# A spectral layer in 32 units: the inverse transform's last two chunks are moved behind the next unit's first transform

## The reference, cut to what matters

```python
xf = jnp.fft.rfft2(x, axes=(1, 2), norm='ortho')              # x: (4, 128, 128, 768)
xr, xi = xf.real, xf.imag                                     # split in 8 blocks of 96 channels
o1r = relu(xr @ w1[0] - xi @ w1[1] + b1[0])                   # per block, 96x96
o1i = relu(xi @ w1[0] + xr @ w1[1] + b1[1])
o2r = o1r @ w2[0] - o1i @ w2[1] + b2[0]
o2i = o1i @ w2[0] + o1r @ w2[1] + b2[1]
o = softshrink(stack(o2r, o2i), 0.01)
out = jnp.fft.irfft2(o, s=(128, 128), norm='ortho') + x
```

## Time and profile before

| | |
|---|---|
| time, median of 3 runs | 5289.3 us (5289.18 to 5289.44) |
| the profiled execution | 5295.64 us, its span 5293.8 us |
| TensorE matmuls busy | 5047.7 us, 95% of the span |
| VectorE, ScalarE, GpSimd busy | 73%, 56%, 27% |
| mean granted TensorE clock | 0.984 of full |
| the 16 DMA engines | 36% of the span on data |

### The profile page before, as it was taken

How to read it: one execution, slowest core, us unless ns; L and a number is a source line. 1 busy time by engine, 2 the same in 40 slices (tenths; PEclk the granted TensorE clock), 3 DMA queues, 4 the chain that set the end, 5 groups by cost and what they waited for, 6 DMA issues and landing times.

```text
span 5293.8 us, 113159 instructions
## 1 busy us (share of the span) xinstructions
PE 5047.7 (95%) x40128; PEld 4731.8 (89%) x40128; DVE 3859.0 (73%) x6195; ACT 2978.4 (56%) x5384; POOL 1434.6 (27%) x905
## 2 busy tenths in 40 slices
PE   6999999999999999999999999999999999999997
PEld 5999889998899988999989998999998999988996
DVE  4777777777777777777767777777777777777775
ACT  4555655556555556555565555655556655556553
POOL 3033312333123332233331233312333223332120
PEclk8999999999999999999999999999999999999998
DMA  4034432344323444223443234432334422344322
GB/s 109 16 87 101 101 71 53 80 101 101 82 55 79 89 101 100 54 64 86 101 102 68 57 82 98 101 79 61 76 89 101 95 58 65 86 101 101 71 67 61
DMA packets 1699963, 430.22 MB, mean 81 GB/s; under 512 B 1699104, under 2 KB 1699232, under 8 KB 1699360
## 3 DMA queue, kind: packets, MB, share of 16 engines
q1 hardware_dynamic: 1699360, 422.47, 36.1%
HBM read 220.89 MB, written 201.33 MB: 80 GB/s over the span
## 4 chain that ended last, share of the span: by engine, by line
PE 90%; DVE 6%; issue 2%; ACT 1%; SPq 1%; DMA 0%; DVEq 0%; ACTq 0%
PE psum L768 15%; PE psum L742 14%; PE psum L818 13%; PE psum L791 13%; PE psum L724 10%; PE psum L801 9%; PE psum L754 7%; PE psum L830 3%; PE psum L831 3%; PE psum L832 3%; DVE spectrum L633 1%; DVE spectrum L632 1%; DVE mixed L654 1%; DVE x L691 1%; SPq L361 1%
## 5 line engine op out<-in xcount | busy, mean ns | idle before, releaser
L654 DVE COPY mixed<-psum 128x768 f32<-128x768 f32 (+1 forms) x544 | 508.1, 934 | 838.5 <-PE psum L754 838.5
L742 PE MATMUL psum<-w_whole,whole 128*128 128x192 f32 x4160 | 796.6, 334 | 110.1 <-ACT whole L480 101.5
L544 ACT ACTIVATE sums_high<-psum 128x512 fp32r<-128x512 f32 x768 | 458.9, 597 | 727.2 <-PE psum L818 727.2
L768 PEld LDWEIGHTS psum<-mats,mixed 128*128 128x128 f32 x6272 | 744.0, 191 | 121.2 <-issue 112.0
L768 PE MATMUL psum<-mats,mixed 128*128 128x128 f32 x6272 | 841.8, 283 | 0.0
L742 PEld LDWEIGHTS psum<-w_whole,whole 128*128 128x128 f32 x4160 | 684.2, 200 | 130.9 <-ACT whole L480 107.6
L724 PE MATMUL psum<-mats,x 128*128 128x128 f32 x6144 | 725.3, 280 | 65.3 <-DVE spectrum L633 28.7
L724 PEld LDWEIGHTS psum<-mats,x 128*128 128x128 f32 x6144 | 713.0, 196 | 75.7 <-DVE spectrum L633 28.9
L791 PE MATMUL psum<-w2t,hidden 128*128 128x192 f32 x4160 | 768.2, 327 | 0.0
L818 PE MATMUL psum<-mats,spectrum 128*128 128x128 f32 x6144 | 743.4, 275 | 13.2 <-DVE spectrum L661 13.2
L818 PEld LDWEIGHTS psum<-mats,spectrum 128*128 128x128 f32 x6144 | 714.2, 192 | 15.6 <-DVE spectrum L661 15.6
(11 more groups left out here) (83 smaller groups left out, 7491.9 us busy)
## 6 DMA issues: line engine op xcount, KB each, us to landing
x<-x SPq DMA_DIRECT2D x736, 192.0 KB, 2.8
out<-x SPq DMA_DIRECT2D x736, 192.0 KB, 2.4
x<-x SPq DMA_DIRECT2D x736, 64.0 KB, 2.6
out<-x SPq DMA_DIRECT2D x736, 64.0 KB, 2.2
x<-x SPq DMA_DIRECT2D x32, 144.0 KB, 2.7
w2t<-L_conv_w SPq DMA_DIRECT2D x128, 36.0 KB
out<-x SPq DMA_DIRECT2D x32, 144.0 KB, 2.3
x<-x SPq DMA_DIRECT2D x64, 48.0 KB, 2.2
```

The source lines that it names most:

```text
L654: dve.tensor_copy(mixed[s % 2][:, 0:k], both_b(s)[:, 0:k]).then_inc(b_copied, 1)
L742: pe.matmul(bank_b(s, k), whole[s % 2][:, k // 2, :, k % 2], w1_whole[par][:, :, :].rearrange("p r o -> p (r o)"), start=k % 2 == 0, stop= ...
L768: last = pe.matmul(out[tile], flat[:, tile * SIZE:(tile + 1) * SIZE], mat(FH), start=True, stop=True)
```

## The change

Chunks 22 and 23 of stage F are issued after the next unit's stage A and not before it. They go into banks 2 and 3, and VectorE adds them after it has emptied stage A's last group and made its share of the gather. Stage A's group 2 therefore no longer comes after F's chunk 23; it waits for the add of chunk 20, whose bank (7) it now takes, since the banks of stage A are turned by one. Groups 4 and 5 wait for `sums_low` of chunks 22 and 23.

Group 21 of stage A is copied out by ScalarE (13 groups, 26 copies) and no longer by VectorE (11 groups). Of the four last gather copies, the one that ScalarE did second is done by VectorE, at the same time as ScalarE does the first.

The loops turn at other places. TensorE does stage A of unit 0 ahead of its loop; its body begins with the layers, so it turns between F's chunk 23 and stage B. ScalarE and VectorE do stage A and the layers of unit 0 ahead of theirs; their body begins with the inverse, so they turn between the layers and the inverse. All three bodies hold four units and turn seven times, and the last units stand behind. All units but the last now have two groups of the next stage A ahead of their stage E.

```diff
+LATE = 2
+NF = NQ - LATE
+A_ACT = [at for at in range(NA) if at % 2 == 0 or at == NA - 3]
+A_DVE = [at for at in range(NA) if at not in A_ACT]
         def bank_a(at):
-            return bank(2 + at if at < AHEAD else 4 + at % 4)
+            return bank(2 + at if at < AHEAD else 4 + (at + 1) % 4)
         def bank_f(q):
-            return bank(F_BANKS[q % len(F_BANKS)] if q < NQ - 1 else 0)...
+            return bank(F_BANKS[q % len(F_BANKS)] if q < NF else 2 + q - NF)...
# ScalarE, gather(0)
-                    act.activation(w[0:BLOCK, :, slice(*INNER)], parts[0:BLOCK, 0], ACT.Copy)
-                    act.activation(w[BLOCK:SIZE, :, slice(*INNER)], parts[HALF:BLOCK, 1], ACT.Copy).then_inc(whole_gathered, 1)
+                    act.activation(w[0:BLOCK, :, slice(*INNER)], first_parts(*INNER)[0:BLOCK, 0], ACT.Copy).then_inc(whole_gathered, 1)
# VectorE, end of stage A
+                dve.tensor_copy(whole[0][BLOCK:SIZE, :, slice(*INNER)], parts[HALF:BLOCK, 1]).then_inc(early_gathered, 1)
                 dve.tensor_copy(halved[0][0:HALF, slice(*INNER)], parts[0:HALF, 1, 0])
                 dve.tensor_copy(halved[0][HALF:SIZE, slice(*INNER)], parts[0:HALF, 1, 1]).then_inc(first_halved, 1)
# VectorE (ScalarE has the same order, without the adds)
+            def forward_next(n, m, par):
+                forward(n)
+                for q in range(NF, NQ):
+                    add(1 - par, n - 1, q)
+            def body(loop, unit, last=False):
...
+                inverse(1 - par, n - 1)
+                forward_next(n, m, par)
+                layers(m, par, n, False, last)
# TensorE, stage_a
-                    if at == 3:
-                        pe.wait_ge(f_added, n * NQ)
+                    elif end_of is not None and at == AHEAD:
+                        pe.wait_ge(f_added, end_of * NF + (NF - 1))
+                    elif end_of is not None and at > AHEAD + 1:
+                        pe.wait_ge(low_copied, end_of * NQ + (NQ + at - AHEAD - 3))
# TensorE, stage_c
+                if s == 0:
+                    pe.wait_ge(f_late_added, n * LATE)
# TensorE, stage_f
-                if q == NQ - 1:
-                    pe.wait_ge(f_added, n * NQ + (NQ - 2))
-                elif q >= len(F_BANKS):
-                    pe.wait_ge(f_added, n * NQ + (q - len(F_BANKS) + 1))
+                if len(F_BANKS) <= q < NF:
+                    pe.wait_ge(f_added, n * NF + (q - len(F_BANKS) + 1))
+            def late(n):
+                for q in range(NF, NQ):
+                    stage_f(n, q)
+            def body(loop, unit):
...
+                layers(par, n)
+                stage_a(m + par, 1 - par, n + 1, 0, AHEAD)
+                inverse(n)
+                stage_a(m + par, 1 - par, n + 1, AHEAD, NA, end_of=n)
+                late(n)
+            stage_a(0, 0, 0, 0, NA)
+            with pe.Fori(0, PAIRS // UNROLL - 1) as loop:
                 for unit in range(2 * UNROLL):
...
+                    body(loop, unit)
+            for unit in range(2 * UNROLL - 1):
+                body(PAIRS // UNROLL - 1, unit)
+            layers(1, UNITS - 1)
+            inverse(UNITS - 1)
+            late(UNITS - 1)
```

More of the change, by code:

```diff
@@ L494, in gather @@
                 act.activation(h[HALF:SIZE], parts[0:HALF, 1, 1], ACT.Copy).then_inc(halved_gathered, 1)
-            with act.Fori(0, PAIRS // UNROLL) as loop:
-                for unit in range(2 * UNROLL):
[L498 to L544, removed]
@@ new lines, in inverse @@
+            def inverse(n):
+                for q in range(NQ):
+                    act.wait_ge(e_done, n * NQ + (q + 1))
+                    act.activation(sums_high[:, q % RING], bank_e(q), ACT.Copy).then_inc(high_copied, 1)
+            def body(loop, unit, last=False):
+                m, par = loop * UNROLL + (unit + 1) // 2, (unit + 1) % 2
+                n = m * 2 + par
+                inverse(n - 1)
+                forward(n)
+                layers(m, par, n)
+            forward(0)
@@ L546, in _ @@
+            layers(0, 0, 0)
+            with act.Fori(0, PAIRS // UNROLL - 1) as loop:
+                for unit in range(2 * UNROLL):
+                    body(loop, unit)
+            for unit in range(2 * UNROLL - 1):
+                body(PAIRS // UNROLL - 1, unit, last=unit == 2 * UNROLL - 2)
+            inverse(UNITS - 1)
         @block.vector
@@ new lines, in layers @@
+            def layers(m, par, n, first, last):
+                for s in range(NS + 2):
+                    if s < NS:
+                        k = pairs(s)
+                        dve.wait_ge(b_done, n * NS + (s + 1))
+                        dve.tensor_copy(mixed[s % 2][:, 0:k], both_b(s)[:, 0:k]).then_inc(b_copied, 1)
+                    for stage in ("sums", "tiles") if s < NS else ("tiles", "sums"):
+                        if stage == "sums" and s >= 2:
+                            t, rows = s - 2, rows_d(s - 2)
+                            j = 2 + 2 * GROUPS[t][0]
+                            dst = real_kw[:, :, :] if t == REAL else U[:, 0:BLOCK, j:j + rows]
+                            dve.wait_ge(excess_done, n * NS + (t + 1))
+                            dve.scalar_tensor_tensor(dst, parts_d(t), LAMBDA, excess[:, :, 0:rows], op0=ALU.add,
+                                                     op1=ALU.min).then_inc(shrunk, 1)
+                        if stage == "tiles" and 1 <= s <= NS:
+                            t = s - 1
+                            dve.wait_ge(c_done, n * NS + (t + 1))
+                            dve.tensor_scalar(middle[t % 2][:, 0:pairs(t)], middle_c[:, 0:pairs(t)], b1t[par][:, 1:2], 0.0,
+                                              ALU.add, ALU.max).then_inc(middle_done, 1)
+                    if 2 <= s < NS:
+                        k = rows_d(s) // 2
+                        dve.wait_ge(shrunk, n * NS + (s - 1))
+                        dve.tensor_copy(bank_d(s).rearrange("p (k r) c -> p k r c", r=2)[:, 0:k],
+                                        b2_rows[par][:, :, :].unsqueeze(1).broadcast_to([SIZE, k, 2, BLOCK])).then_inc(seeded, 1)
+                    if s < 2 * NP and not first:
+                        unfold_step(n - 1, 1 - par, s)
+                    if 2 * NP <= s < 2 * NP + PREPARE and not last:
+                        prepare_step(m + par, 1 - par, s - 2 * NP)
@@ new lines, in inverse @@
+            def inverse(par, n):
+                for batch in range(0, NQ, BATCH):
+                    for q in range(batch, batch + BATCH):
+                        dve.wait_ge(high_copied, n * NQ + (q + 1))
+                        dve.tensor_tensor(sums_low[:, q % RING], bank_e(q), sums_high[:, q % RING],
+                                          ALU.subtract).then_inc(low_copied, 1)
+                    for q in range(batch - BATCH, batch):
+                        if q >= 0:
+                            add(par, n, q)
@@ L698, in _, with body @@
+            def forward_next(n, m, par):
+                forward(n)
+                for q in range(NF, NQ):
+                    add(1 - par, n - 1, q)
+            def body(loop, unit, last=False):
+                m, par = loop * UNROLL + (unit + 1) // 2, (unit + 1) % 2
+                n = m * 2 + par
+                inverse(1 - par, n - 1)
+                forward_next(n, m, par)
+                layers(m, par, n, False, last)
             for k in range(PREPARE):
                 prepare_step(0, 0, k)
-            turn(0, first=True)
@@ L701, in _ @@
-            with dve.Fori(1, PAIRS // UNROLL - 1) as loop:
-                turn(loop)
-            turn(PAIRS // UNROLL - 1, last=True)
+            forward(0)
+            layers(0, 0, 0, True, False)
+            with dve.Fori(0, PAIRS // UNROLL - 1) as loop:
+                for unit in range(2 * UNROLL):
+                    body(loop, unit)
+            for unit in range(2 * UNROLL - 1):
+                body(PAIRS // UNROLL - 1, unit, last=unit == 2 * UNROLL - 2)
+            inverse(1, UNITS - 1)
@@ L704, in _ @@
+            for q in range(NF, NQ):
+                add(1, UNITS - 1, q)
             for k in range(2 * NP):
@@ L710, in mat, with stage_a @@
                 return mats[:, columns]
-            def stage_a(m, par, n, first, end):
+            def stage_a(m, par, n, first, end, end_of=None):
                 for at, g in list(enumerate(A_ORDER))[first:end]:
@@ L833, in stage_f, with layers, inverse @@
                 last.then_inc(f_done, 1)
+            def layers(par, n):
+                for s in range(NS + 2):
+                    if s < NS:
+                        stage_b_whole(par, n, s)
+                    if s == NS:
+                        flip(n)
+                        stage_c(n, NS - 1)
+                    if s >= 2:
+                        stage_d_outer(par, n, s - 2)
+                        stage_d_middle(par, n, s - 2)
+                    if s < NS:
+                        stage_b_halved(par, n, s)
+                    if 1 <= s < NS:
```

(16 more changed lines are left out.)

193 lines of the change are left out of this document (87 added, 106 removed).

## The result

The changed kernel takes 5331.0 us (median of 4 runs, 5328.8 to 5332.0) against 5289.2 us: the ratio is 1.0079, with an interval of [1.0062, 1.0097], so it is slower by 0.8%. The forecast was 5158 us, and the range went to 5200. So 173 us are to be found.

The account below looks back on a forecast made before the run. TensorE was taken as the bound, so only its waits and lower clock could be won: 83.7 (turns) + 23.5 (clock) + 49 - 27 (loops) + 1.2 + 0.5 (ends) = 131 us off 5289.3, giving 5158; range 5135 to 5200.

Parts of the forecast that it names:

- a turn within the body: From F's chunk 22 to the next stage B: 22.85 us in place of 25.55, 2.70 saved 31 times, 83.7 us.
- The clock: After the gaps before stage B: no more falls to 1.2 GHz, 16 x 1.47 = 23.5 us saved.
- Rival 3: VectorE's late adds, beside GpSimd's halving, delay the layers' first `mixed` copy: slower, 5298 us if 5 us late; chance 0.03.
- the late adds: VectorE's adds of F's late chunks, behind the gather: done about 3.8 us after stage A, 0.5 us of cover left.
- Rival 2: The gap before stage B stays 3.17 us, late F fills 1.4, the clock holds: 5197 us, chance 0.13.
- The late chunks: F's last two chunks, 1.40 us, hide fully in the 1.91 before stage B; group 2 starts after 0.91.
- Group 21 on ScalarE: At stage A's end VectorE is free for group 23, which is out 1.44 us after stage A.
- The loops' turns: Seven old turns at 7.0 us saved, 49 us; six new ones at 2.5 + 1.3 + 0.7 paid, 27 us.
- The 0.7 for the clock: At each of six new loop turns, a 3.03 us gap lets the clock fall half the time: half of 1.47.
- The sum: Whole kernel: 83.7 + 23.5 + 49 - 27 + 1.2 + 0.5 = 131 us saved, giving 5158 us.

Follow-up runs that it names:

- e1: Changed kernel with the second of the last gather copies back on ScalarE; all else of the change stays: 5151.3 us, ratio 0.9735 to the kernel before.
- e2: Changed kernel with GpSimd's halving made to wait until VectorE's gather copy is done: 5140.0 us, ratio 0.9714 to the kernel before.
- e4: Changed kernel with GpSimd's halving cut into two instructions of half the rows: 5169.5 us, ratio 0.9770 to the kernel before.
- e6: Changed kernel with VectorE's 32x132 gather copy made as two copies of 32x66 beside the halving: 5142.4 us, ratio 0.9716 to the kernel before.
- e5: Kernel before with one thing changed, the second of ScalarE's last two gather copies moved to VectorE: 5409.2 us, ratio 1.0223.
- e9: Changed kernel with the halving put off, and F's chunks 22 and 23 back ahead of stage A: 5227.6 us, ratio 0.9879 to the kernel before.
- e8: Changed kernel with the halving put off, and group 21 of stage A back on VectorE: 5166.4 us, ratio 0.9770 to the kernel before.
- e10: Kernel before with the loops alone turned in the new places, all else of the change left out: 5228.1 us, ratio 0.9883.

## Why the prediction was wrong

- **The step that failed** is in the part on a turn within the body: "Then one gather copy of 0.32 in place of two", and with it "stage B can start at 1.44 + 0.10 + 0.32 + 0.05 = 1.91". I priced the half on VectorE by ScalarE's rows, as "at most 0.32 each". Alone it is 0.22 us, better than that. But it stood 4.01 us, and the start was 1.40 + 4.20 = 5.6. Shown by e1, e2, e4, e6 and, in the kernel before, e5.
- **The clock** then turned the sign. TensorE waits 136.3 us before stage B; in e2, whose two rows follow, 25.1. That is 111 us. The changed kernel is 191 us slower than e2, so the other 80, 2.5 a unit, are the half clock after the gap (2.7 was the estimate from 29 against 47 matmuls); TensorE is busy 5083.8 us against 5003.0, the same 80. The forecast had 23.5 us won by the clock, since gaps of 0.75 and 0.5 should let it fall nowhere. That rule held: in e2 it falls after no gap before stage B.

```profile
PE psum L786 <- ACT whole L486: 13.3, 26, 1.9
PE psum L786 <- ACT whole L479: 11.8, 6, 2.2
```

- **Rival 3** named the place, VectorE behind GpSimd's halving, and got 0.03. It looked at the wrong instructions: the late adds. These take 0.55 and 0.28 us beside the halving too (e6, at 546.27 to 547.68, inside 544.03 to 549.34), and TensorE waits for them in no run that has them behind stage A. Its argument against was copies of 0.69 us inside the halving. Those read PSUM, and say nothing on a copy from SBUF to SBUF.
- **Rival 2** said that the clock holds when only 1.8 us are idle. e9 shows that it does not: it falls after 16 of 21 gaps of 1.83 or 1.84 us.
- **The trace of before had shown it.** Two small VectorE instructions of one shape each, whose duration ranges sevenfold and fivefold, beside GpSimd's fold steps of 1.5 to 1.8 us. In 26 of the 32 units each of the two is long, and each long one ends 0.11 or 0.21 us after a fold step that was running when it began. A third, the TENSOR_SCALAR on `w2t` (L605), ranges from 0.19 to 1.88 us, again ending with a fold step. The prediction drew on none of them. Minimum, median and maximum of the first two in the kernel before:

```profile
L609 DVE CAST b_high<-b2t x32: 250/740/1729, 49.7 to 5047.2; 1x192 fp32r<-1x192 f32 x32
L612 DVE TENSOR_TENSOR b_parts<-b2t,b_high x32: 348/813/1785, 50.0 to 5052.4; 1x192 fp32r<-1x192 f32 x32
```

- **The late chunks** were right: they hide in full, and group 2 waits 0.66 us. Taking them back (e9) costs 88 us, of which 45 were expected; the rest is the clock.
- **Group 21 on ScalarE** was right: e8, 26 us for the 1.0 us by which VectorE ends later.
- **The loops' turns** were right in sign, and the price of the new ones was too high, 27 us. (For E, the prediction's own rows give 1.2 late and not 1.3.) ScalarE's and VectorE's cost E 0.3 us, not 1.3. ScalarE's table load is gone (it ran eight times before, and once now), and its idle time is hidden; VectorE begins E's first `sums_low` 0.4 us late. At a turn, E's 32 matmuls take 4.06 us against 3.74, and ScalarE starts after 1.91 idle against 1.92. ScalarE's loads, and the turn itself:

```profile
L506 ACT ACT_TABLE_LOAD x1 | 1.3, 1283 | 0.7 <-PEq L937 0.7
```

```profile
832.96 4.06 PE L864 MATMUL psum<-mats,spectrum 128*128 128x128 f32 x32
...
835.12 2.04 DVE L708 TENSOR_TENSOR sums_low<-psum,sums_high 128x512 fp32r<-128x512 f32 x3 [2.60 <-ACT sums_high L544]
...
834.06 0.60 ACT L544 ACTIVATE sums_high<-psum 128x512 fp32r<-128x512 f32 x1 [1.91 <-PE psum L864]
```

  TensorE's is hidden behind the 4.2 us; in e2 it is the second of the two rows above, 11.8 us in six turns: 1.97 where 0.43 is normal, 1.5 us more and not 2.5. That row names ScalarE's L479, but stage B's first group waits for L486 and VectorE's copies, and not for L479: the time is TensorE's own turn. With 0.3 for E the six turns cost 11 us and not 27. The 0.7 for the clock was paid at none of the six in e2, at one in e6 and at three in e1.
- **The sum** for what was meant, a copy that doesn't wait, was 5158. e2 and e6 measure it: 5140 and 5142, both 2.8 to 2.9% under the kernel before, and the best versions here. The 16 us that the turns cost less are most of the 18 between 5158 and 5140.

## What to carry to other kernels

Before work goes to VectorE, look at what GpSimd does at that moment, and ask of the new instruction whether it is of a kind that waited here: a copy or scalar operation within SBUF that takes two elements per step, or an instruction with two SBUF inputs. If so, its price has the rest of GpSimd's running instruction on top. A cheap witness is in the trace already: an instruction of one shape whose maximum is several times its minimum. And price a longer gap on TensorE twice, by its own length and by the clock after it: here they were 111 and 80 us. The cures are small: start the GpSimd instruction later, cut it in pieces, or give the copy a form that takes one element per step.

## What the runs showed of the hardware

- The same VectorE copy of 32x132 elements takes 0.22 us with GpSimd silent, 4.01 when it comes 1.4 us into an instruction of 5.31 us, 3.02 when it comes later into it (e5), and 1.45 into one of 2.7 (e4), while copies of 32x66 never wait (0.204 to 0.216 us, 64 of them, e6).
- The wait also meets a TENSOR_TENSOR with two SBUF inputs (0.18 to 1.93 us in e2), and not copies from PSUM (0.69) or an add with one input in PSUM (0.55, inside the halving in e6).
- The granted clock can fall after an idle gap of 1.84 us (e9: 0.76 in the unit's first 7 us, after 16 of 21 such gaps) and stay up after the next one of the same length. It falls after none of the gaps of 1.63 to 1.65 us in e4 or of 1.39 to 1.42 in e8. After gaps of 3.1 to 3.3 us it falls in 16 of 32 units in the kernel before and in 6 of 32 in e10; after gaps of 4.2 us or more, in every unit of the changed kernel, and for longer (0.60).
- ScalarE reloaded its table in each turn of its loop when no ScalarE instruction stood ahead of the loop (8 loads of 1.28 us), and once in all when stage A of unit 0 did.
